# A CIN kernel on one core: the square features get their own partitions and are added for two slabs at a time

## The reference: what is computed

```
def _cin_layer(x0, x, kernel):            # x0 (2048, 32, 32)
    W = kernel.reshape(m, h_prev, kernel.shape[1])
    return jnp.einsum('bmd,bhd,mho->bod', x0, x, W)
x = x0
for k in (k1, k2, k3):                     # k1 (32*32, 32), k2 (32*32, 128), k3 (32*128, 64)
    x = _cin_layer(x0, x, k)
    finals.append(jnp.sum(x, axis=-1))
logit = jnp.concatenate(finals, axis=-1) @ kf   # (2048, 1)
```

## Time and profile before

| | |
|---|---|
| median of 3 runs | 315.96 us (315.61 to 316.22) |
| profiled execution, its own time | 314.67 us |
| its span | 312.8 us |
| PE busy | 299.8 us, 96% |
| GpSimd busy | 221.6 us, 71% |
| VectorE busy | 198.2 us, 63% |
| ScalarE busy | 183.8 us, 59% |
| bytes moved | 86.86 MB, mean 278 GB/s |
| mean granted TensorE clock | 0.995 |

### The profile page before, as it was taken

The page is one execution under the profiler, slowest core; times in us unless marked ns, Lnnn a source line. Parts: engine busy times, 40 slices in busy tenths (PEclk is TensorE's granted clock), DMA queues, the critical chain, the costliest instruction groups (busy, mean ns, idle before and its releaser), DMA issues.

```text
span 312.8 us, 7671 instructions
## 1 busy us (share of the span) xinstructions
PE 299.8 (96%) x3020; PEld 82.7 (26%) x3022; DVE 198.2 (63%) x221; ACT 183.8 (59%) x195; POOL 221.6 (71%) x130
## 2 busy tenths in 40 slices
PE   7689699999999999999999999999999999999995
PEld 2133122222222222222222222222222222222221
DVE  0673856776666667776666666776666666777631
ACT  1326465776665566776666566676666566676611
POOL 0333697878777777978777777888777777888700
PEclk9999799999999999999999999999999999999999
DMA  6969999999999998888777777888777777611010
GB/s 200 321 211 396 334 383 381 386 354 368 358 370 346 322 322 295 322 333 311 299 297 280 274 282 295 316 327 310 301 300 285 272 282 294 270 36 35 1 36 1
DMA packets 18665, 86.86 MB, mean 278 GB/s; under 512 B 3932, under 2 KB 4188, under 8 KB 9692
## 3 DMA queue, kind: packets, MB, share of 16 engines
q1 hardware_dynamic: 15864, 77.84, 66.2%
q10 hardware_dynamic: 2756, 8.84, 10.3%
q0 software_dynamic: 32, 0.00, 0.0%
HBM read 86.14 MB, written 0.53 MB: 277 GB/s over the span
## 4 chain that ended last, share of the span: by engine, by line
PE 84%; DMA 9%; SPq 2%; POOL 2%; ACT 1%; DVE 1%; issue 0%; POOLq 0%
PE acc L556 67%; PE acc L562 10%; PE rot L539 7%; DMA v<-v_rows 5%; DMA xc<-x_chunks 2%; DMA t_tab<-ts 2%; POOL prod L369 2%; SPq L216 1%; ACT split L288 0%; POOL split L377 0%; POOL low L375 0%; SPq L211 0%; SPq L233 0%; DVE low L431 0%; SPq L234 0%
## 5 line engine op out<-in xcount | busy, mean ns | idle before, releaser
L556 PE MATMUL acc<-prod,w 128*32 128x512 f32 x2048 | 227.7, 595 | 0.9 <-POOL prod L369 0.9
L369 POOL TENSOR_TENSOR prod<-u,v 128x1024 f32<-128x1024 f32 x64 | 151.8, 2393 | 40.4 <-PE acc L562 28.6
L556 PEld LDWEIGHTS acc<-prod,w 128*32 128x32 f32 x2048 | 63.0, 110 | 148.4 <-issue 145.4
L478 DVE TENSOR_TENSOR xy<-acc,ysb 128x512 f32<-128x512 f32 x32 | 22.1, 692 | 91.0 <-ACT ysb L293 91.0
L270 ACT ACTIVATE prod<-rot 128x1024 f32<-128x1024 f32 x64 | 65.6, 1025 | 22.7 <-DVE prod L472 15.9
L472 DVE TENSOR_TENSOR prod<-rot,u 128x1024 f32<-128x1024 f32 x64 | 77.8, 1216 | 1.4 <-DMA v<-v_rows 1.3
L472 DVE TENSOR_TENSOR prod<-rot,v 128x1024 f32<-128x1024 f32 x64 | 77.8, 1216 | 0.0
L293 ACT ACTIVATE ysb<-acc,kf 128x512 f32<-128x512 f32 x32 | 22.0, 687 | 73.6 <-PE acc L562 73.6
L274 ACT ACTIVATE feat<-u 128x2048 f32<-128x2048 f32 x32 | 61.0, 1907 | 2.1 <-DMA v<-v_rows 2.1
L377 POOL TENSOR_TENSOR split<-low,split 128x512 bf16<-128x512 f32 x30 | 34.8, 1160 | 23.2 <-ACT split L288 23.2
L562 PE MATMUL acc<-feat,wf 64*32 64x512 f32 x512 | 35.0, 603 | 2.3 <-issue 2.3
(11 more groups left out here) (37 smaller groups left out, 26.7 us busy)
## 6 DMA issues: line engine op xcount, KB each, us to landing
u<-u_rows SPq DMA_DIRECT2D x31, 1024.0 KB, 4.9
v<-v_rows SPq DMA_DIRECT2D x31, 1024.0 KB, 6.9
xc<-x_chunks SPq DMA_DIRECT2D x32, 256.0 KB, 7.2
feat<-u_rows ACTq DMA_DIRECT2D x32, 256.0 KB, 3.2
u<-k3p SPq DMA_DIRECT2D x4, 256.0 KB, 4.9
u<-u_rows SPq DMA_DIRECT2D x2, 512.0 KB, 6.5
v<-v_rows SPq DMA_DIRECT2D x2, 512.0 KB, 7.1
v<-k2t SPq DMA_DIRECT2D x1, 512.0 KB, 6.4
```

Of the source, the lines that this page charges most:

```text
L369: nc.gpsimd.tensor_tensor(prod[p][:, UV, pair(half)], us[n][:, pair(half)], vs[n][:, pair(half)], ALU.mult).then_inc(uv_ready, 2)
L478: nc.vector.tensor_tensor(xy[p][:], acc[p][0][:], ysb[p][:], ALU.mult).then_inc(xy_ready, 1)
L556: nc.tensor.matmul(acc[p][h][quad(c), :], w[:, t, h * G:(h + 1) * G], prod[p][:, t, chunk(c)], start=(t == first), stop=False, skip_group_ ...
```

## The change

Four edits that belong together.

1. The plain fields get partitions of their own, the last 32 (`quad(3)`); the squaring writes only partitions 0 to 95 (`FEATS`). So the DMA of the fields no longer waits for the squares. `place_fields(s+1)` moves from behind the second half of WW to right behind `take_y(s-1)`, ahead of the first half of WW, and waits for `acc_ready` of slab s-1 in place of `feat_ready`.
2. The weights `wf` of the features move with them: the folded squares of h = 0 to `quad(0)` and of h = 1 to `quad(2)`, the linear row to `quad(3)`; half h = 0 of `features` now uses rows 0 to 63, h = 1 rows 64 to 127.
3. TensorE in an odd step s adds the features of slab s, and right behind them those of slab s+1 into the other pair of banks, where they are the first matmuls of their sums (`opens=True`). In an even step there are no features: the contraction adds to what the features have begun, and its own last matmul raises `acc_ready`.
4. Before the last tile (VW of h = 1) of an odd step, TensorE waits for `feat_ready` and the fields of slab s as before, and now also for `xy_ready` of slab s-1, and for the squares and the fields of slab s+1.

```
             def square_fields(s, p, n):
                 wait(act, acc_ready, s - 1)
-                nc.scalar.activation(feat[p][:], us[n][:], ACT.Square).then_inc(feat_ready, 1)
+                nc.scalar.activation(feat[p][FEATS, :], us[n][FEATS, :], ACT.Square).then_inc(feat_ready, 1)
             def place_fields(s, p):
-                act.wait_ge(feat_ready, s + 1)
-                act.dma_start(feat[p][quad(1), :], fields).then_inc(feat_in[p], 16)
+                wait(act, acc_ready, s - 1)
+                act.dma_start(feat[p][quad(3), :], fields).then_inc(feat_in[p], 16)
...
                 if not isinstance(s, int) or s + 1 < SLABS:
+                    place_fields(s + 1, q)
                     act.wait_ge(rot_ready, s + 2)
-                    wait(act, acc_ready, s)
                     square_w(s + 1, q, 0)
...
                     square_w(s + 1, q, 1)
-                    place_fields(s + 1, q)
...
+            def features(p, opens=False):
+                for h, rows in enumerate((slice(0, 2 * M), slice(2 * M, 4 * M))):
                     for c in range(CHUNKS):
+                        mm = nc.tensor.matmul(acc[p][h][quad(c), :], wf[rows, :], feat[p][rows, chunk(c)], start=opens,
+                                              stop=not opens, skip_group_check=True)
+                if not opens:
+                    mm.then_inc(acc_ready, 1)
...
+                tiles = (UV, WW, UW, VW)
                 wait(pe, xy_ready, s - 1)
-                for h in range(2):
-                    contract(s, h, p, (UV, WW, UW, VW), UV, 32 * it + 16 * (n // 2 + 1))
+                if n % 2 == 0:
+                    contract(s, 0, p, tiles, None)
+                    contract(s, 1, p, tiles, None).then_inc(acc_ready, 1)
+                    return
+                contract(s, 0, p, tiles, UV)
+                contract(s, 1, p, tiles[:-1], UV)
+                pe.wait_ge(feat_ready, s + 1)
+                pe.wait_ge(feat_in[p], 32 * it + 16 * (n // 2 + 1))
+                more = not isinstance(s, int) or s + 1 < SLABS
+                if more:
+                    pe.wait_ge(xy_ready, s)
+                    pe.wait_ge(feat_ready, s + 2)
+                    pe.wait_ge(feat_in[1 - p], 32 * it + 16 * ((n + 1) // 2 + 1))
+                contract(s, 1, p, tiles[-1:], UV)
                 features(p)
+                if more:
+                    features(1 - p, opens=True)
```

More of the change, by code:

```diff
@@ L39 @@
 HALFWAY = slice((Q - 1) * M, P)
+FEATS = slice(0, (Q - 1) * M)
 def index(pair, q, i):
@@ L119, in cin_kernel @@
         tr = sb("tr", [P, TILES, G])
-        td = sb("td", [M, G])
+        td = sb("td", [P, G])
         w = sb("w", [P, TILES, 2 * G])
@@ L137, in cin_kernel @@
         fixes_ps = [acc[1][h][:, 0:2 * G].rearrange("p (n g) -> p n g", g=G) for h in range(2)]
-        fold_ps = [acc[1][0][2 * M:3 * M, 2 * G:3 * G], acc[1][1][0:M, 2 * G:3 * G]]
+        fold_ps = [acc[1][0][0:M, 2 * G:3 * G], acc[1][1][2 * M:3 * M, 2 * G:3 * G]]
         k2_in, kf2_in, kf1_in = (sem(n) for n in ("k2_in", "kf2_in", "kf1_in"))
@@ L320, in _ @@
             act.wait_ge(cleared, 1)
-            act.dma_start(wf[quad(1), :], ts[M:M + 1, :]).then_inc(lin_in, 16)
+            act.dma_start(wf[quad(3), :], ts[M:M + 1, :]).then_inc(lin_in, 16)
             for half in range(2):
@@ L387, in _ @@
             pool.wait_ge(t_out, 32)
-            pool.dma_start(td[:], bass.AP(tensor=t_tab.tensor, offset=0,
+            pool.dma_start(td[quad(2), :], bass.AP(tensor=t_tab.tensor, offset=0,
                                           ap=[[(WRAP + 1) * G, M], [1, G]])).then_inc(td_in, 16)
@@ L493, in _ @@
             split_low(1)
-            fold_squares(0, quad(2), k1s[quad(2), 2 * TILES, :])
+            fold_squares(0, quad(0), k1s[quad(0), 2 * TILES, :])
             multiply_w(0, 0, 0, (0,))
@@ L505, in _ @@
             dve.wait_ge(td_in, 16)
-            fold_squares(1, quad(0), td[:])
+            fold_squares(1, quad(2), td[quad(2), :])
             def step(it, n):
@@ L541, in rotate, with contract @@
                 mm.then_inc(rot_ready, 1)
-            def contract(s, h, p, tiles, first, count=None):
+            def contract(s, h, p, tiles, first):
                 for t in tiles:
@@ L551, in contract @@
                         pe.wait_ge(products_ready, 4 * s + (3 if t == UW else 4))
-                    if h == 1 and t == VW and count is not None:
-                        pe.wait_ge(feat_ready, s + 1)
-                        pe.wait_ge(feat_in[p], count)
                     for c in range(CHUNKS):
[L556 to L560, removed]
+                        mm = nc.tensor.matmul(acc[p][h][quad(c), :], w[:, t, h * G:(h + 1) * G], prod[p][:, t, chunk(c)],
+                                              start=(t == first), stop=(first is None and t == tiles[-1]),
+                                              skip_group_check=True)
+                return mm
+            def features(p, opens=False):
+                for h, rows in enumerate((slice(0, 2 * M), slice(2 * M, 4 * M))):
                     for c in range(CHUNKS):
-                        mm = nc.tensor.matmul(acc[p][h][quad(c), :], wf[rows, :], feat[p][rows, chunk(c)], start=False,
-                                              stop=True, skip_group_check=True)
-                mm.then_inc(acc_ready, 1)
+                        mm = nc.tensor.matmul(acc[p][h][quad(c), :], wf[rows, :], feat[p][rows, chunk(c)], start=opens,
+                                              stop=not opens, skip_group_check=True)
+                if not opens:
+                    mm.then_inc(acc_ready, 1)
             def fixes_of(h):
```

## The result

The changed kernel takes 322.84 us, the median of 6 runs (319.72 to 323.55), beside 315.75 us for the kernel before (6 runs, 315.03 to 316.22): 1.0218 of it, 95% interval 1.0188 to 1.0247. I had forecast 318.0 with a range up to 321.0. The direction was right, the size was not: 7.1 us were lost where I had worked out 2.0. The profiled execution took 322.75 us, span 321.0.

A forecast was written before the change was run, and what follows sets the result against it. PE, busy 96% of the span, was taken to bound the kernel. Gains of 2.2 and 0.2 us against stalls of 2.4 and 2.0 made it 2.0 us slower: 315.96 to 318.0 us, range 313.3 to 321.0.

The forecast's parts named there:

- Changes of weight shape: On PE, two steps have five changes in place of six; 0.15 us gained per even slab, 1.95 us for slabs 4 to 28.
- slab 30's: At the end, no rotation follows slab 30's features and the contraction comes directly: 0.28 us gained.
- Rival 4: Direct step from contraction to rotation costs PE as much as the two it replaces; only the start gains: 320.2 us, chance 0.04.
- The wait and where it stands: PE waits in odd steps before h = 1's last tile, due +6.77, fields requested +0.3; stall is landing time less 6.37.
- the full part: Until about 115 us DMA engines are full; odd steps 3 to 9 stall 0.6 us each, 2.4 us (0.5 to 4.8).
- The later odd steps: Odd steps 11 to 29, ten of them, stall 0.2 us each for the next slab's fields, 2.0 us together.
- Rival 1: Fields land as late in the ten later odd steps as in the full part: 6.0 us lost, 322.0 us, chance 0.10.
- The start: Slab 2's features fill PE's hole before the rotation at 45.79, early fields delay loads: gain 0.2 us (-0.5 to +1.0).
- Rivals 2 and 3: 2: fields land ahead of `v`, only early stalls, 316.0 us, chance 0.27; 3: stalls none or under 0.1, 313.6 us, 0.15.
- Rival 2: In later bursts fields slip in behind `u`, ahead of `v`, landing +4 to +5, no stall there: 316.0 us, chance 0.27.

The follow-up runs named there:

- both repairs: Changed kernel, even slabs' fields asked for one step earlier and those of slabs 0 and 1 behind their squares: 312.34 us, 0.9873; on another chip 312.90 us, 0.9915.
- the kernel without pairs: Changed kernel with early requests and own partitions kept, but every step adds its own features behind its own contraction: 318.27 us, 1.0075 of the kernel before.
- the first: Changed kernel with only the even slabs' fields asked for one step earlier, behind the even step's rotation: 315.97 us, 0.9993 of the kernel before.
- the four kernels above: Kernel before (315.75 us), changed kernel (322.84), and the changed kernel with fields written to a spare tile's 128 partitions (316.83) or every fourth partition (314.41).

## Why the prediction was wrong in size

**Changes of weight shape: right.** I took 0.15 us for a pair; the pairs without a stall are 17.40 us in place of 17.56, and so they are in the kernels with both repairs. The other part of the gain, slab 30's, is in the last stretch. Rival 4 fell.

**The wait and where it stands: right.** The place, what is behind it, the due time of +6.77 and the request at +0.3 (0.26 measured) came out, and PE stalled in 12 of 14 odd steps. The size in the full part was close: 2.9 us for the 2.4 that I took.

**The later odd steps: wrong, 4.8 us for 2.0.** The failed step is "the burst ends at about +6, so that the last packets are alone. I take 0.2 each". Both nearest rows that I named said 0.4 over the limit, and I went below them on an argument. The argument left out that the fields slow the burst that they are in: `v` lands after 8.6 us in place of 6.8, so the burst ends later than I reckoned. In the step shown above the queues read so, first from 164.5 to 169.9 us, then from 169.9 to 171.9 (q1 is SyncE's queue, q10 ScalarE's; packets, MB, share of 16 engines):

```profile
q1 hardware_dynamic: 212, 1.61, 77.9%
...
DMA packets 69, 0.57 MB, mean 283 GB/s; under 512 B 0, under 2 KB 0, under 8 KB 0
...
q1 hardware_dynamic: 37, 0.30, 58.3%
q10 hardware_dynamic: 32, 0.26, 49.3%
```

The first packet of the fields goes some 3.7 us after the request, and then the two queues share 283 GB/s for 2 us; the fields land at 173.3. Their packets are not alone, as I had reckoned for the last ones. Rival 1 (0.6 each, 6.0 us) was nearer, and its 322.0 is near the measured 322.84, but for half the reason: it had the start as a gain.

**The start: wrong, and by as much.** I had a gain of 0.2, with -0.5 as the lower bound; 2.4 to 3.6 us were lost (the kernel without pairs, and both repairs against the first). What the medians leave is 2.0 (7.1 less the 7.7 of stalls, with the 2.6 that the shapes gained). The failed step is "256 KB at 420 GB/s is 0.6 us of delay". That prices bytes at the rate of a load into 128 partitions, and those of one request where two go out early. The trace of before has the row for the right price: the second one here, a stretch in which the fields are alone in flight, beside one of loads alone.

```profile
161.00:164.00 3.00, 3.00 (x32) 0.91 (x28) 2.86 (x4) 3.00 (x3) 3.00 (x2) 1.00 1.03 434
165.75:167.00 1.25, 1.25 (x16) 0.39 (x12) 1.15 (x2) 0.63 (x1) 0.51 (x2) 1.00 0.82 210
```

210 GB/s against 434, at four fifths of the engines' time. At 210 GB/s two requests are 2.5 us of the queue, an estimate from that row, ahead of the load of `v` for slab 1 that the start of the changed kernel hangs on, where in the kernel before most of them came behind it. From the issue of `u` to GpSimd's first product of slab 1 it took 12.4 us in the changed kernel, 9.2 in the one before, and 9.4 and 10.5 with the fields in 128 and in every fourth partition. "SBUF — State Buffer", Door 1: The DMA port swizzle, in the Trainium skill says that 32 or 64 neighbouring partitions reach only 8 of 16 ports and so get half the bandwidth, while bit 6 of the partition number picks the other eight. The trace agrees: half the rate for partitions 32 to 63 alone (210 GB/s); with the loads beside, 235 to 314 for partitions 96 to 127, and 411 to 427 for 128 partitions and for every fourth one, which has both values of that bit. That the loads beside such a request slow down as well is shown by the rates of the four kernels above. The prediction uses neither that row nor that page.

**Rivals 2 and 3 fell.** The fields did not slip in ahead of `v`: asked for at +0.26, they sent their first packet at about +4.0, when 1.6 MB of the loads had gone, as much as `u` and half of `v`, and landed at +7.3. Rival 2 also had 0.6 us for their bytes, where they took 2.0. Only two pairs have no stall: the third, where the landing took 6.4 us, and the last, whose request meets no more loads.

What stays open: why 128 rows of 2 KB land later in the loop than 32 rows of 8 KB in every fourth partition; and, of the start, how its cost divides between the late load and the slower clock behind the longer gap (both are in each execution, and executions of one kernel differ by 3 us there).

## What to carry to other kernels

A request that is made earlier isn't one that lands earlier: look at what is in flight at the new moment, take the landing time from a row of that moment, and compare it with the time at which it is due. Price a DMA at the rate of its own destination shape, not at that of the big loads beside it; a busy share near 1 with a falling GB/s is the sign (1.05 at 235 GB/s here, 0.99 at 418). And when a wait is added to the engine that sets the end, ask for the data a whole step earlier if its buffer is free then: here that alone took the kernel from 1.0218 to 0.9993 of the time before, and with the first two requests back behind their squares it gains 0.9% to 1.3%.

## What the hardware showed unexpectedly

DMAs of 256 KB into 32 neighbouring partitions take bandwidth from the loads in flight beside them: 235 to 314 GB/s together, against 418 to 427 with the same rows in every fourth partition, at a DMA share of 1.05 and 1.06 against 0.99 and 1.04. One queue shows it as well as two (262 GB/s with the requests in line in SyncE's queue).
